# A clear in front of each indirect DMA: one word on 16 partitions in place of 64 words on 64

## The reference

```python
edge_index = jnp.stack([src, dst])
x = _layernorm(x + _L0_gnn_ref(x, edge_weight, edge_attr_3, edge_index, ...))   # relu(w @ w1 + b1) @ w2, tensor product with x[src], summed at dst
x = _layernorm(x + _L1_gnn_ref(x, edge_index))                                  # 3 hops of norm * x[src], summed at dst, mean of the hops
x = _layernorm(x + _L2_gnn_ref(x, edge_index, edge_attr_32, ...))               # MLP of [x[src], x[dst], attr], maximum at dst
x = _layernorm(x + _L3_gnn_ref(x, edge_attr3_2x32, src, dst, ...))              # attention: softmax over a destination's edges, summed at dst
```

## Time and profile before

| | |
|---|---|
| median of the runs | 1860.24 us |
| span of the profiled execution (the page gives no other time of it) | 1863.2 us |
| POOL busy | 1400.9 us, 75% |
| DVE busy | 1344.3 us, 72% |
| PE, ACT busy | 729.3 us, 488.0 us |
| DMA moved | 114.29 MB, 61 GB/s on average |

### The profile page before, as it was taken

The page is one execution under the profiler, slowest core; times in us unless marked ns, Lnnn a source line. Parts: engine busy times, 40 slices in busy tenths (PEclk is TensorE's granted clock), DMA queues, the critical chain, the costliest instruction groups (busy, mean ns, idle before and its releaser), DMA issues.

```text
span 1863.2 us, 14783 instructions
## 1 busy us (share of the span) xinstructions
PE 729.3 (39%) x3676; PEld 546.2 (29%) x3676; DVE 1344.3 (72%) x2600; ACT 488.0 (26%) x1014; POOL 1400.9 (75%) x2019
## 2 busy tenths in 40 slices
PE   7912555541450003605337001456605656551400
PEld 3301222220220003605326001355505655551400
DVE  9955999986999645775755882478785999986400
ACT  7822311110110013522334200233302343342100
POOL 8878887888888885868878558884068888888776
PEclk9966778775785556867678555677757776665655
DMA  8165511111111101412222330000001111110000
GB/s 321 38 211 194 184 32 32 32 26 17 26 20 50 42 20 59 137 65 76 99 88 102 140 137 4 5 23 13 30 20 24 32 28 26 32 29 9 10 10 10
DMA packets 64097, 114.29 MB, mean 61 GB/s; under 512 B 27599, under 2 KB 48648, under 8 KB 63224
## 3 DMA queue, kind: packets, MB, share of 16 engines
q1 hardware_dynamic: 24304, 80.96, 12.0%
q0 software_dynamic: 33728, 12.79, 4.9%
q10 hardware_dynamic: 5960, 19.43, 2.8%
HBM read 61.66 MB, written 55.21 MB: 63 GB/s over the span
## 4 chain that ended last, share of the span: by engine, by line
POOL 75%; issue 17%; DVE 5%; PE 1%; DMA 1%; ACT 0%; POOLq 0%; SPq 0%; DVEq 0%
POOL A_dst L746 12%; POOL A_src L746 12%; POOL out L880 12%; POOL gtmp L736 9%; POOL work L746 8%; POOL A_msg L746 7%; POOL A_msg L823 7%; POOL edge_sums L829 5%; POOL out_short L746 3%; DVE A_dst L1484 1%; DVE stat L1495 1%; DVE work L2276 0%; DVE A_sum L1484 0%; PE bank L1388 0%; DVE A_dst L1492 0%
## 5 line engine op out<-in xcount | busy, mean ns | idle before, releaser
L746 POOL DMA_INDIRECT A_dst<-in_x,dst_i x196 | 224.3, 1144 | 57.4 <-POOL gtmp L736 39.1
L736 POOL MEMSET gtmp<- 64x64 f32 x934 | 156.5, 168 | 144.6 <-DMA table<-A_dst 110.9
L880 POOL DMA_INDIRECT out<-A_dst,out_i x196 | 217.9, 1112 | 59.7 <-POOL gtmp L736 34.3
L1495 DVE TENSOR_REDUCE work<-work 128x80 f32<-128x1280 f32 (+3 forms) x147 | 204.6, 1421 | 78.8 <-issue 50.2
L1310 PE MATMUL bank<-w2fold,work 128*128 128x384 f32 x392 | 183.1, 611 | 173.0 <-DVE work L1484 162.7
L746 POOL DMA_INDIRECT A_src<-x_pos,A_tmp x140 | 147.2, 1051 | 40.5 <-POOL gtmp L736 24.4
L746 POOL DMA_INDIRECT work<-table,pos_i x112 | 144.9, 1294 | 31.1 <-POOL gtmp L736 23.5
L1235 PE MATMUL bank<-ident,work 128*128 128x128 f32 (+1 forms) x294 | 63.4, 327 | 264.1 <-ACTq L995 139.2
L1310 PEld LDWEIGHTS bank<-w2fold,work 128*128 128x128 f32 x392 | 86.0, 237 | 269.5 <-issue 227.1
L746 POOL DMA_INDIRECT A_msg<-table,pos_i x112 | 139.0, 1241 | 32.4 <-POOL gtmp L736 16.5
L1484 DVE TENSOR_TENSOR work<-bank,work 128x384 f32<-128x384 f32 (+1 forms) x294 | 153.6, 590 | 0.2
(11 more groups left out here) (396 smaller groups left out, 2335.5 us busy)
## 6 DMA issues: line engine op xcount, KB each, us to landing
work<-in_x SPq DMA_DIRECT2D x26, 960.0 KB
x_pos<-A_sum SPq DMA_DIRECT2D x13, 990.0 KB
out<-work ACTq DMA_DIRECT2D x13, 960.0 KB
A_tmp<-ew_turned_rows ACTq DMA_DIRECT2D x49, 130.0 KB
table<-A_dst SPq DMA_DIRECT2D x2, 3136.0 KB
edge_sums<-A_dst SPq DMA_DIRECT2D x2, 3136.0 KB
table<-A_dst SPq DMA_DIRECT2D x13, 448.0 KB
A_tmp<-in_edge_attr_2x SPq DMA_DIRECT2D x49, 112.0 KB
```

The lines of the kernel that those rows point to most:

```text
L736: pool.memset(tile, 0.0).then_inc(cleared, 1)
L746: pool.indirect_dma_start(out=column(t), out_offset=None, in_=of, in_offset=bass.IndirectOffsetOnAxis(ap=idx[:, t:t + 1], axis=0), bounds_ ...
L880: pool.indirect_dma_start(out=out, out_offset=bass.IndirectOffsetOnAxis(ap=out_i[:, t:t + 1], axis=0), in_=A_dst[:, t, :], in_offset=None, ...
L1495: return v.tensor_reduce(out=o, in_=a, axis=AX, op=op)
```

## The change

Each of the calls that place a clear is given another piece of the tile `gtmp`: `gtmp[0:HF]` is 64 partitions by 64 words of float32, `gtmp[0:16, 0:1]` is 16 partitions by 1 word. There are 7 such places in the code, and 934 clears when it runs. The count of clears, the semaphore and the wait stay.

```diff
             gather(lambda t: pos_x[:, t:t + 1], pos_table, src_i, node_limit, lambda t: pos_rows, range(plain),
-                   cleared_tile=gtmp[0:HF])
+                   cleared_tile=gtmp[0:16, 0:1])
...
-                   range(plain, T), cleared_tile=gtmp[0:HF])
-            gather_dst(range(DST_FIRST * GATHER_CHUNK, T), None, gtmp[0:HF])
+                   range(plain, T), cleared_tile=gtmp[0:16, 0:1])
+            gather_dst(range(DST_FIRST * GATHER_CHUNK, T), None, gtmp[0:16, 0:1])
...
                         pool.wait_ge(n_out, keep(t))
-                    pause(gtmp[0:HF])
+                    pause(gtmp[0:16, 0:1])
                     move(t).then_inc(done, 16)
...
                 for t in range(FEWEST2):
-                    pause(gtmp[0:HF])
+                    pause(gtmp[0:16, 0:1])
                     move(t).then_inc(hop_done, 16)
...
-                           range(c * GATHER_CHUNK, c * GATHER_CHUNK + SLOTS_IN_WINDOW), cleared_tile=gtmp[0:HF])
+                           range(c * GATHER_CHUNK, c * GATHER_CHUNK + SLOTS_IN_WINDOW), cleared_tile=gtmp[0:16, 0:1])
...
                     if i < 6:
-                        pause(gtmp[0:HF])
+                        pause(gtmp[0:16, 0:1])
```

## The result

The changed kernel takes 1947.57 us (median of 4, 1942.95 to 1967.89), the kernel before 1857.65 (median of 4). The ratio is 1.0499, with an interval of 1.0446 to 1.0551: **5% slower**, where 1813 us was forecast.

The account below looks back on a forecast made before the run. POOL was taken to bound the kernel, with 75% of the chain. 934 clears x 55 ns = 51.4 us, less 3, 0.5 and 0.5, gave 47.4 off 1863.2, or 1815.8; as a median 1813 us, range 1785 to 1840.

Parts of the forecast that it names:

- The price of the words: In each of POOL's 934 clears, writing 63 words less saves 54 ns.
- The price of the partitions: In each of POOL's clears, going from 64 to 16 partitions saves nothing.
- hand-over: 21 ns of the median clear, put down to the DMA ahead of it and taken to stay.
- rival A: POOL's clear all but goes, 77 ns or more each: about 1792 us, down to 1733; chance 0.15.
- Term (a): POOL's indirect DMAs, started more often, meet DVE instructions 4% more often: 3 us of the gain lost.
- the 3% allowed: Sign to check in the profile after: mean times of the indirect DMAs stay within 3% of now.
- the opposite one: A shorter gap leaves DVE less room to get in first: some 3 us more gained, left out of the sum.
- part (b): At POOL's long waits DVE has slack, so the gain counts in full, except 0.5 us from 835 to 934 us.
- rival C: DVE and the stores keep part of POOL's gain; with half of it lost, 1835 us; chance 0.16.
- Rival D: Slower: with a shorter gap POOL's gathers fall into step with DVE, 0.35 us lost each, 1890 us; chance 0.07.

Follow-up runs that it names:

- chip D: Fourth group of follow-up runs, on one chip or session: the changed kernel took 1766.0 us there, the kernel before 1856.5.
- A: First group of follow-up runs, on one chip or session: the kernel before took 1859.7 us there; the changed kernel wasn't run.
- i1: Neither clear nor wait ahead of any indirect DMA, against the kernel before: 2279.3 us, ratio 1.2208, on E.
- e1: Changed kernel with its clear on 64 partitions by 1 word: 1790.7 us, 0.9624 of the kernel before, on A.
- B: Second group of follow-up runs, on one chip or session: the changed kernel took 1967 us there, the kernel before 1861.9.
- C: Third group of follow-up runs, on one chip or session: the changed kernel took 1995.5 us there, the kernel before 1862.5.
- E: Fifth group of follow-up runs, on one chip or session: the changed kernel took 2013.3 us there, the kernel before 1864.1.
- g3: Changed kernel with its clear on 16 partitions by 64 words: 1883.3 us, 1.0144 of the kernel before, on C.
- g4: Changed kernel with its clear on 16 partitions by 16 words: 1889.0 us, 1.0183 of the kernel before, on C.
- h1: Neither clear nor wait ahead of any indirect DMA, against the kernel before: 1718.9 us, ratio 0.9262, on chip D.
- h2: The changed kernel itself, run again: 1766.0 us, 0.9505 of the kernel before, on chip D.
- e2: Changed kernel with its clear on 16 partitions by 64 words: 1813.2 us, 0.9756 of the kernel before, on A.
- f3: Changed kernel with its one-word clear on partitions 32 to 47: 1909.7 us, 1.0255 of the kernel before, on B.
- h4: Changed kernel with clears on changing words and a wait only ahead of every 64th: 1719.6 us, 0.9266 of the kernel before, on chip D.

## Why the prediction was wrong

**The price of the words** was right: 54 ns forecast, 52 to 53 measured.

**The price of the partitions** was wrong. "I take nothing for going from 64 to 16" rested on the earlier trace rows, 65 partitions against 128, both of clears that stood behind other clears. Behind an indirect DMA the 48 partitions cost 24 ns, which is the 21 ns that the prediction called hand-over and left in place. The clear fell by 77 ns, as rival A said, and the beat by 86 (1441 to 1355), since the indirect DMA behind it fell from 1003 to 995 ns in the median as well. Rival A's reason, that the work of 16 partitions "may be done beside the end of the DMA", fits, but what happens inside isn't shown. The Trainium skill, page "GPSIMD Engine Reference", section "Instruction dispatch", says that an instruction completes when all eight cores are done, and gives no price for partitions. That fewer of them save nothing was the prediction's inference from it, and the 24 ns measured for 16 against 64 contradict this inference.

**The indirect DMAs.** Term (a) had them 3 us longer. They read shorter: from before's trace to the one on chip D POOL's clears fell by 71.8 us, its indirect DMAs by 35.7 (mean 1170 to 1134 ns, so just over the 3% allowed) and its idle time rose by 10.4, 97.1 us less together, of the span's 98.5. But this sets two chips side by side, for before has no profile on A or D. Among the eight traces of A and D, with beats from 1301 to 1416 ns, the mean is 1132 to 1150 ns and doesn't follow the beat (1133 to 1145 at 1301, 1134 at 1355, 1150 at 1380, 1132 at 1412, 1147 at 1416). It falls with the beat only where increments are late, from 1170 in before to 1102 in after and 1082 in i1. So neither the sign of term (a) nor the opposite one, which the prediction took from the "SBUF — State Buffer" page of the Trainium skill, is borne out: between 1301 and 1416 ns no effect of the beat is seen.

**The other engines.** On chip D part (b) held in the main: POOL waits longest for the table store, 78.2 us against 78.9 in the earlier trace rows, and DVE's destination rows now keep it 6.8 us in 2 pieces, 6.2 of it at the start of the final scatter, a small form of rival C. The gain there was 90 us where 47.4 was forecast. Of the 43 us more, 934 x 0.024 = 22 are the partitions; the rest is not told apart, since before lies some 20 us above what the other kernels' beats give (below). On the first measurement's chip it failed, and this is the step that turned the sign. The prediction had named the sign for it: "If the beat falls as I say and the time doesn't, (b) is wrong". The beat fell by more than it said and the time rose. Part (b) asks whether DVE still has slack once POOL is earlier, and takes the duration of everything that DVE, PE and ACT do as given. "No other engine reads or waits on a clear" is true and was the trap: the clear acted on them through the pace that it gave POOL. The gap of 0.17 us between two indirect DMAs held the beat at 1440 ns, where the late increments cost next to nothing. At 1355 ns they are 470 us in sum, of which some 180 us (1947.6 - 1766.0) reached the end; that is an estimate, as the two times are of two chips.

**Rival D** had the sign, and its heading, "the clear is what keeps DVE out of the way", the wrong mechanism: the gathers' medians stayed at 1.00 us, and DVE's busy time at 1343.5 us. That it came out slower, as D said, is luck.

Could the trace of before have told? In part. The kernel's longest group in the earlier trace rows shows 57.4 us of idle time with "POOL gtmp L736" as the releaser of 39.1. In every trace from chips A and D with a clear and its wait, that is 48.9 or 49.0 of 57.4 or 57.5; e1's row:

```profile
L746 POOL DMA_INDIRECT A_dst<-in_x,dst_i x196 | 223.6, 1141 | 57.4 <-POOL gtmp L736 48.9 <-issue 8.5
```

The rest is put down to "issue" because semaphore records are missing. A trace from A or D holds 24,575 to 25,541 of them; before had 19,699, after 13,157 and i1 11,021. Before had also six groups of waits on a "remote", 15 waits and 18.5 us, in a program of one core, the largest of them here. The eight traces of A and D have none:

```profile
ACT small L1006 <- remote: 6.8, 5, 3.1
```

I read the size of this row and not that on one core it should not exist. They would not have given the price, but a chance of a slower end above 0.07.

**What stays open.** Why chips B, C and E (and the first one) have late increments and A and D don't, and whether it is the chip at all or the session. Whether the rate alone orders the time: on C it doesn't (g3, g4), though it orders the late waits on line 1310. And what is overrun: lost records and late increments always came together here, and on the whole, the fewer records a trace holds, the more waits on PE are over 2 us late (19,699 with 16, 16,145 with 48, 13,157 with 82, 11,021 with 143), so the recording itself may be what delays PE. Every timed run here carries a span and a clock from a recording, so whether the kernel is slower without one is not known. And the kernel before lies some 20 us above the line of time over mean beat through h1, h2, e1 and e2 even on A and D, where it has no profile.

## What to carry to other kernels

Work that nobody waits for can still be the pace of a stream. Before taking such a gap out of a dense run of indirect DMAs, ask what else each of them sends (here 16 increments every 1.4 us; that they are what holds PE's increments up isn't shown), and measure on more than one chip: the kernel before is within 0.5% on all five, the kernel with no clear is 7% faster on two of them and 22% slower on a third. Where every chip is of the kind of A and D, the one with no clear is the best. Of the versions that ran on both kinds only the clear of one word on 64 partitions was never slower than before: 0.9624 on A and 0.9875 on C, the second within the 2% that count as the same. And experiments that are to explain a run have to stand beside that run, on its chip: the first four here were read wrongly until the changed kernel and two of them ran side by side.

## What the runs showed of the hardware

- A clear of 16 partitions by 1 word behind an indirect DMA takes 88 ns, of 64 by 1 113, of 16 by 64 141, of 64 by 64 165, of 16 by 96 168. A word costs 0.8 ns.
- On partitions 32 to 47 it takes 90 ns (f3), on 0 to 15 88.
- With its wait a clear of 88 ns costs 54 ns of beat (1355 - 1301), without the wait none (h4). Without a clear 0.30 us lie between two indirect DMAs, behind a clear with its wait 0.27.
- On some chips an increment of TensorE's semaphore comes up to 17 us late (after), 32 us (i1) or 38 us (g3) while GpSimd issues an indirect DMA every 1.30 to 1.41 us. ACT's increments are on time within 0.01 us in all of these traces, VectorE's are over 0.3 us late in 25 waits of after.
- In the stage of line 1310 such lateness was seen at beats of 1384 ns and less and not at 1415 ns and more, in twelve traces.
